# Attention scores on F32R row strips, with both first-pass chunks of a slot back to back

## The reference

```python
mod = (silu(c) @ wmod)                      # shift, scale, gate of each half
h = layernorm(x) * (1 + ca) + sa
x = x + ga * attention0(h, k0, v0, Wq, Wo)  # 16 heads of 16, 1024 queries, 4096 given keys
h = layernorm(x) * (1 + cb) + sb
x = x + gb * experts_low(h)
# second layer, modulated again
h = layernorm(x) * (1 + ca) + sa
x = x + ga * attention1(h, Wqkv, Wproj)     # 16 heads of 16, 1024 queries, 1024 keys made from h
x = x + gb * (wide attention and experts of high precision)(h)

scores = einsum('bqhd,khd->bhqk', Q, K) * SCALE
out = einsum('bhqk,khd->bqhd', softmax(scores), V)
```

## Time and profile before

| | us |
|---|---|
| runs: median, lowest, highest of 3 | 2120.23, 2119.72, 2126.68 |
| the profiled execution, by the clock of the runs | 2117.09 |
| its span in the trace | 2115.3 |
| a0's block | 69.1 to 886.4 |
| a1's block | 1035.3 to 1287 |

### The profile page before, as it was taken

One profiled execution on the slowest core, in us unless ns is written; L12 is line 12 of the kernel. 1 busy time (PEld: TensorE's weight loads), 2 busy tenths in 40 slices (PEclk: granted clock), 3 DMA queues, 4 the chain that ended last, 5 costly groups with the idle time before them and its releaser, 6 DMA issues. The chain is left out here.

```text
span 2115.3 us, 31356 instructions
## 1 busy us (share of the span) xinstructions
PE 1808.1 (85%) x9772; PEld 970.4 (46%) x9772; DVE 1399.7 (66%) x1846; ACT 1147.7 (54%) x2253; POOL 285.7 (14%) x447
## 2 busy tenths in 40 slices
PE   4499999999999999645699973499999999949997
PEld 3122222222222233133222221388888888748886
DVE  6487777877777888246467753666666666656665
ACT  3067767776777777513377762255445454424432
POOL 3210000000000000102111111211111111002223
PEclk8599999999999999856799986799999999979999
DMA  7201111111111200112312222100000000023432
GB/s 284 96 34 35 40 46 35 41 39 36 35 39 35 89 16 16 36 56 55 112 65 70 72 101 73 39 14 20 7 20 20 20 12 10 1 51 115 121 105 65
DMA packets 56274, 115.00 MB, mean 54 GB/s; under 512 B 7249, under 2 KB 21585, under 8 KB 54123
## 3 DMA queue, kind: packets, MB, share of 16 engines
q1 hardware_dynamic: 53715, 109.21, 15.9%
q10 hardware_dynamic: 2456, 4.46, 0.8%
HBM read 83.52 MB, written 30.12 MB: 54 GB/s over the span
## 5 line engine op out<-in xcount | busy, mean ns | idle before, releaser
L348 DVE TENSOR_REDUCE a_max_part<-psum 128x1 f32<-128x1024 f32 x640 | 759.6, 1220 | 253.8 <-PE psum L265 253.8
L389 ACT ACTIVATE a_probs<-psum 128x512 f32<-128x512 f32 x1280 | 675.1, 603 | 247.9 <-PE psum L309 242.7
L265 PE MATMUL psum<-a_k_rows,a_q_rows 96*128 96x512 bf16 x1280 | 399.6, 395 | 52.0 <-DMA a_q_rows<-q_parts 26.1
L309 PE MATMUL psum<-a_q_rows,a_k_rows 99*128 99x512 bf16 x1280 | 410.3, 386 | 29.6 <-ACT a_probs L389 29.3
L300 PE MATMUL psum<-a_probs,a_v_ext 128*32 128x512 f32 x2560 | 342.5, 607 | 6.1 <-ACT a_o_out L373 3.8
L265 PEld LDWEIGHTS psum<-a_k_rows,a_q_rows 96*128 96x128 bf16 x1280 | 98.8, 98 | 407.0 <-issue 193.0
L309 PEld LDWEIGHTS psum<-a_q_rows,a_k_rows 99*128 99x128 bf16 x1280 | 124.1, 98 | 268.8 <-ACT a_probs L389 155.4
L1548 PE MATMUL psum<-high_t_parts,high_gu 128*128 128x512 f32 x600 | 145.6, 393 | 6.8 <-DVE high_t_parts L1642 6.8
L1253 PE MATMUL psum<-wide_k_t,wide_q_t 128*128 128x512 f32 (+3 forms) x576 | 130.3, 353 | 1.7 <-DVE wide_id_bf L1452 1.7
L1548 PEld LDWEIGHTS psum<-high_t_parts,high_gu 128*128 128x128 f32 x600 | 113.6, 190 | 31.3 <-issue 7.3
L226 POOL TENSOR_TENSOR a_max_bf<-a_neg_max,a_zeros 128x4 bf16<-128x4 f32 x64 | 13.2, 206 | 849.0 <-DVE a_neg_max L352 849.0
(11 more groups left out here) (173 smaller groups left out, 1871.1 us busy)
## 6 DMA issues: line engine op xcount, KB each, us to landing
o<-a_o_out SPq DMA_DIRECT2D x64, 256.0 KB, 2.1
gu_in<-in_w_gu SPq DMA_DIRECT2D x25, 256.0 KB, 3.0
k_parts<-keys_parts SPq DMA_DIRECT2D x12, 512.0 KB, 6.5
a_k_rows<-k_parts SPq DMA_DIRECT2D x16, 384.0 KB
high_cw<-cw SPq DMA_DIRECT2D x24, 256.0 KB, 3.9
setup_k_in<-in_k SPq DMA_DIRECT2D x4, 1024.0 KB, 15.2
a_k_rows<-k_parts SPq DMA_DIRECT2D x16, 256.0 KB
a_v_in<-in_v SPq DMA_DIRECT2D x16, 256.0 KB, 14.8
```

The costliest lines, as they stand in the source:

```text
L265: mm = pe.matmul(psum[:, 2 * (n % 2) + j, :], q_rows[0:KROWS, b, q0:q0 + P], k_rows[0:KROWS, b, k0:k0 + 512], start=True, stop=True)
L309: pe.matmul(psum[:, bank_of(filling(j)), :], k_rows[0:SROWS, b, j * P:(j + 1) * P], q_rows[0:SROWS, b, half * QH:(half + 1) * QH], start=T ...
L348: dve.tensor_reduce(max_part[:, u % 2, c // nch, c % nch:c % nch + 1], psum[:, 2 * (n % 2):2 * (n % 2) + 2, :], AX.XY, ALU.max).then_inc(s ...
L389: act.activation(probs[:, j % pring, :], psum[:, bank_of(filling(j)), :], ACT.Exp).then_inc(exp_done, 1)
```

## The change

q and k are now held in the type F32R, in words of four bytes: each number is a high part and the rest, and three products are kept, 3 x 16 = 48 rows, with 3 rows of maxima 51. That fits twice into the array's 128 rows: strip 0 is rows 0 to 50, strip 1 rows 64 to 114, and q stands in both. Strip 0 holds the first half of the keys, strip 1 the other. A first-pass chunk is two matmuls, one on each strip (`first_half(n, 0)`, `first_half(n, 1)`); second scores take the strips in turn, j even on strip 0 and j odd on strip 1.

The order of a slot becomes S S F F S S PV. `shift` is 6 and `turn_at` 6 before the last, and the loops are unrolled. The sums are taken by VectorE instead of ScalarE, before the third reduction of the next unit. The row of maxima is written by ScalarE to a buffer of its own, and SP sends it to both strips with two DMAs. The keys come as fp32 (four DMAs a head, one for each strip's two high copies and one for its low rows) into a single buffer `k_in` and are split on GpSimd by three operations; setup does this for head 0 beside the modulation, and the split into bf16 with its stores is gone. `project` makes two parts; q stays in SBUF for a0 (`load_q` is six DMAs of 16 rows out of it), for a1 q goes through DRAM in 48 fp32 rows a head (`load_q` two DMAs) and k as it is. `nb` is 3 in a0 and 6 in a1. At unit 29 SP loads back 15 heads' sums, and `merge_heads` loads one.

```diff
+STRIP = 64
+MROWS = 3
+LOW_K, MROW = 32, 48
+SROWS = MROW + MROWS
...
-    shift = 3
-    turn_at = nkt - 2
...
+        self.shift = 6
+        self.turn_at = nkt - 6
...
+    def strip_of(self, j, rows):
+        return slice(STRIP * (j % 2), STRIP * (j % 2) + rows)
...
+    def load_k(self, sp, h):
+        keys = self.k_dram[HD * h:HD * h + HD, :]
+        for n in range(2):
+            part = keys[:, n * self.per_strip:(n + 1) * self.per_strip]
+            at = STRIP * n
+            sp.dma_start(self.k_in[at:at + 2 * HD, :],
+                         part.unsqueeze(0).broadcast_to([2, HD, self.per_strip])).then_inc(self.k_loaded, 16)
+            sp.dma_start(self.k_in[at + LOW_K:at + MROW, :], part).then_inc(self.k_loaded, 16)
...
+    def split_keys(self, pool, h):
...
+        b = h % self.nb
+        pool.wait_ge(self.k_loaded, 64 * (h + 1))
+        pool.tensor_tensor(self.k_rows[:, b, :], self.k_in[:, :], self.zeros[:, 0:1].broadcast_to([P, self.per_strip]),
+                           ALU.add).then_inc(self.k_high, 1)
+        pool.wait_ge(self.k_high, h + 1)
+        for s in range(2):
+            low = slice(STRIP * s + LOW_K, STRIP * s + MROW)
+            pool.tensor_tensor(self.k_rows[low, b, :], self.k_in[low, :], self.k_rows[low, b, :],
+                               ALU.subtract).then_inc(self.k_split, 1)
+        pool.wait_ge(self.k_split, 2 * h + 2)
...
+            def send_maxima(u):
+                b, half = (u // 2) % nb, u % 2
+                sp.wait_ge(self.row_ready, u + 1)
+                for s in range(2):
+                    sp.dma_start(q_rows[STRIP * s + MROW:STRIP * s + SROWS, b, half * QH:(half + 1) * QH].bitcast(F32),
+                                 self.max_row[0:MROWS, u % 2, :]).then_inc(self.rows_loaded[u % 2], 16)
+
+            load_q(sp, q_rows[:, 0, :], 0, self.q_loaded[0])
+            for h in range(1, nb):
+                load_q(sp, q_rows[:, h, :], h, self.q_loaded[h])
+            for h in range(1, self.early + 1):
+                sp.wait_ge(self.k_split, 2 * h)
+                self.load_k(sp, h)
+                sp.wait_ge(self.v_ready, h)
+                self.load_v(sp, h)
+            sent = self.early + 1
+            send_maxima(0)
+            for u in range(us):
+                h, half = u // 2, u % 2
+                if u + 1 < us:
+                    send_maxima(u + 1)
+                sp.wait_ge(self.o_full, u + 1)
+                sp.dma_start(self.o_dram[h, :, half * QH:(half + 1) * QH], self.o_out[:, half, :]).then_inc(self.o_stored[half], 16)
+                if half == 1 and h + nb < H:
+                    load_q(sp, q_rows[:, h % nb, :], h + nb, self.q_loaded[h % nb])
+                while sent < min(H, heads_split(u) + 1):
+                    sp.wait_ge(self.k_split, 2 * sent)
+                    self.load_k(sp, sent)
+                    sp.wait_ge(self.v_ready, sent)
+                    self.load_v(sp, sent)
+                    sent += 1
+                if u == us - 3:
+                    for n in range(2):
+                        sp.wait_ge(self.o_stored[n], 16 * (H - 1))
+                    load_sums(sp, o4, self.o_dram, 0, H - 1, self.o4_loaded)
...
+            for u in range(us):
+                if u + 1 < us:
+                    split_max(u + 1)
+                for h in range(done, heads_split(u)):
+                    self.copy_v(pool, h)
+                    self.split_keys(pool, h)
+                done = heads_split(u)
...
-                for j in range(2):
-                    k0 = ch * 1024 + j * 512
-                    mm = pe.matmul(psum[:, 2 * (n % 2) + j, :], q_rows[0:KROWS, b, q0:q0 + P],
-                                   k_rows[0:KROWS, b, k0:k0 + 512], start=True, stop=True)
-                mm.then_inc(s1_full, 1)
...
+            def first_half(n, s):
...
+                u, c = n // steps, n % steps
+                b, half, qt, ch = (u // 2) % nb, u % 2, c // self.nch, c % self.nch
+                q0, k0 = half * QH + qt * P, ch * 512
+                rows = self.strip_of(s, MROW)
+                return pe.matmul(psum[:, 2 * (n % 2) + s, :], q_rows[rows, b, q0:q0 + P], k_rows[rows, b, k0:k0 + 512],
+                                 start=True, stop=True)
...
+            def second_wait(u, j):
+                bank_free(u, self.filling(j))
+                if j == 0:
+                    pe.wait_ge(self.rows_loaded[u % 2], 32 * (u // 2 + 1))
...
+                k0, rows = (j // 2) * P, self.strip_of(j, SROWS)
+                pe.matmul(psum[:, self.bank_of(self.filling(j)), :], k_rows[rows, b, k0:k0 + P],
+                          q_rows[rows, b, half * QH:(half + 1) * QH], start=True, stop=True).then_inc(self.s2_full, 1)
...
+            def slot(u, g):
...
+                j = group * g
+                one = u * steps + 2 * g + ahead
+                for n in (j, j + 1):
+                    second_wait(u, n)
+                    second_chunk(u, n)
+                for n in (one, one + 1):
+                    if n < self.chunks:
+                        first_wait(n)
+                        first_half(n, 0)
+                        first_half(n, 1).then_inc(self.s1_full, 1)
+                if j + 2 == self.turn_at and u + 1 < us:
+                    turn_maxima(u + 1)
+                for n in (j + 2, j + 3):
+                    second_wait(u, n)
+                    second_chunk(u, n)
+                if g > 0:
+                    pv_group(u, g - 1)
+                elif u > 0:
+                    pv_group(u - 1, groups - 1)
...
+            def take_sums(u):
...
+                half = u % 2
+                dve.wait_ge(self.pv_done, (u + 1) * groups)
+                if u >= 2:
+                    dve.wait_ge(self.o_stored[half], 16 * (u // 2))
+                dve.tensor_copy(self.o_out[:, half, :], psum[:, 7, :]).then_inc(self.o_full, 1)
...
+                for s in range(steps):
+                    if s == 2 and u > 0:
+                        take_sums(u - 1)
+                    n = u * steps + s + ahead
+                    if n < self.chunks:
+                        first_pass_chunk(n)
...
-            def take_sums(it, u):
...
-                half = u % 2
-                act.wait_ge(pv_done, it * (bu * groups) + (u + 1) * groups)
-                act.wait_ge(o_stored[half], it * (16 * nb) + 16 * (u // 2 + 1))
-                act.activation(o_out[:, half, :], psum[:, 7, :], ACT.Copy).then_inc(o_full, 1)
...
+            def put_row(u):
...
+                act.wait_ge(self.turned, u + 1)
+                if u >= 2:
+                    act.wait_ge(self.rows_loaded[u % 2], 32 * (u // 2))
+                act.activation(self.max_row[0:MROWS, u % 2, :], psum[0:MROWS, self.bank_of(self.turn_at), :],
+                               ACT.Copy).then_inc(self.row_ready, 1)
...
+                def load_q(sp, rows, h, loaded):
+                    at = HD * (h % 8)
+                    for n in range(2):
+                        for m, src in enumerate((q_high, q_low, q_high)):
+                            row = STRIP * n + HD * m
+                            sp.dma_start(rows[row:row + HD, :].bitcast(F32), src[at:at + HD, h // 8, :].bitcast(F32)).then_inc(loaded, 16)
...
+                def load_q(sp, rows, h, loaded):
+                    for n in range(2):
+                        sp.dma_start(rows[STRIP * n:STRIP * n + MROW, :].bitcast(F32), q1[h, :, :]).then_inc(loaded, 16)
```

More of the change, by code:

```diff
@@ new lines, in _ @@
+            put_row(0)
+            for u in range(us):
+                for j in range(nkt):
+                    p = u * nkt + j
+                    if j == self.turn_at and u + 1 < us:
+                        put_row(u + 1)
+                    act.wait_ge(self.s2_full, p + 1)
+                    if p >= self.pring and p % group == 0:
+                        act.wait_ge(self.pv_done, (p - self.pring) // group + 1)
+                    act.activation(self.probs[:, p % self.pring, :], psum[:, self.bank_of(self.filling(j)), :],
+                                   ACT.Exp).then_inc(self.exp_done, 1)
@@ new lines, in project, with _ @@
+        if q_out is not None:
+            @block.sync
+            def _(sp):
+                heads = P // HD
+                for c in range(DC):
+                    sp.wait_ge(high_done, 2 * c + 2)
+                    sp.wait_ge(low_done, 2 * c + 2)
+                    for at, src in ((0, q_high), (HD, q_low), (2 * HD, q_high)):
+                        sp.dma_start(q_out[heads * c:heads * (c + 1), at:at + HD, :], src[:, c, :].bitcast(F32)).then_inc(stored, 16)
+                for c in range(DC):
+                    sp.wait_ge(k_taken, 2 * c + 2)
+                    sp.dma_start(k_out[c * P:(c + 1) * P, :], k_sb[:, c, :]).then_inc(stored, 16)
```

565 lines of the change are left out of this document (212 added, 353 removed).

## The result

The changed kernel takes 2273.0 us (median of 4 runs), the kernel before 2120.3: ratio 1.070, 95% interval 1.066 to 1.074. It is slower by 153, where 28 faster were forecast. One of the four runs was disturbed (3000.75) and is left out of the ratio. The two profiled spans, 2268.5 and 2115.3, differ by the same 153.2.

What follows compares the result with a forecast made beforehand. The prediction took PE (TensorE) to bound a0's slot. Its terms, a0 -97, m0 and m1 -8, p1 +2, a1 +75, sum to -28 on the profiled 2117.1: 2092 on the median's scale, range 1998 to 2157.

Steps and rivals of the forecast that it cites:

- a0's start: Front of a0: first chunk near 62.5 instead of 88.6, second scores at 97 instead of 112.2: -15 (-8 to -21).
- The strips overlap: a0's slot on PE: an F32R pair on two strips takes one matmul's time, 0.23, for a unit of 20.9.
- the lower bound by PV's column tiles: a0's slot on PE: 2.4 with pairs side by side, not 2.85, taken since PV's column tiles overlap.
- Rival A: a0's slot on PE: strips run one after another, a unit 23.9 instead of 20.9, +93, 2185; chance 0.12.
- TensorE bounds the slot before: a0's slot in the kernel before: PE is never idle in 2.83 us and sets its length.
- Just in time: a0's rows of maxima through SP: 3 us on the way, about 3.5 between the turn and the unit's end.
- hidden by 20.9: a0's queues: key and q loads stand behind the o store and are covered by a unit's 20.9 us.
- rival B: a1's queue eats a0's gain: starts wait over 10 us, clock falls to 1.2 GHz, a1 +130, 2147; chance 0.15.
- The stall before unit 31: a0's end: 15 heads' sums load at unit 29 ahead of unit 31's maxima, a stall of 18 (4 to 26).
- SP's serial queue: a1's units: maxima wait behind sums, store and loads; with start and sums load a1 loses +75 (+25 to +100).
- m0 gained, p1 lost: Outside the attentions: m0 and m1 together -8 (-10 to -4), p1's q stores +2 (0 to 3).
- The range: Whole kernel: 1998 to 2157, from the ends of the terms for a0, m0 and m1, p1 and a1.

Runs made afterwards that it cites:

- the run with rows first: Changed kernel, but SP sends unit u+2's row of maxima before it waits for unit u's sums: 2130.2 us, 1.004 of the kernel before.
- pacing: GpSimd fetches and splits one head in two units from the start, against the kernel with rows sent first: 2083.2 us, 0.982 of the kernel before.
- GpSimd's order alone: In a1 GpSimd splits a head one unit later, against the 2066.0 us kernel (rows first, paced splits, reordered start): 2010.1 us, 0.949 of the kernel before.

## Why the prediction was wrong

The forecast was 2092, the measured time 181 more. Of these, some 21 lie in a0's start, 14 in its unit (31 times 21.35 instead of 20.9), 49 in late rows and the clock behind them, 9 in a0's last unit, 8 between the attentions, 76 in a1 and 5 behind it.

- **The strips overlap: right.** The slot and the unit came nearly as worked out, 2.61 and 21.35 against 2.53 and 20.9 (20.3 to 21.5). The choice of the lower bound by PV's column tiles held. Rival A is out.
- **TensorE bounds the slot before: half right.** The slot quoted stood in the unrolled last round. In the loop most take 2.91, and 0.08 of each was order, not TensorE. It didn't change the forecast's sum, which went by the period of a unit.
- **a0's start: wrong by 20.** First chunk 69.2 instead of 62.5, second scores 117.6 instead of 97. Head 1's keys, reckoned to land 8 us after their issue, were split from 89.6 to 102.3, behind 18 q loads of 0.6 each, not 0.4. The first maxima stood behind them until 103.6 (PE waited 10.9), and the first row, which I did have queueing behind head 2's keys, was issued at 106.0 and PE waited 12.3 for it.
- **"Just in time" in a0: the step that failed first.** I put the row's way at 3 us within 3.5 of slack, and let the loads be "hidden by 20.9". At 448.2 the way was 6.3 (ScalarE's row at 441.96, two issues of 0.72 instead of 0.4, 4.2 of landing instead of 2.1), and PE left it 4.3. The loads were hidden from the engines and not from the row: it came some 2 late in 13 of 30 units, nearly every second one. The stall's second part, the granted clock at 0.50 for over eight us behind it, was in no term at all; I had it only in rival B, for a1. Together the 30 periods from the second to the last negated maximum cost 689.5, and 30 x 21.35 are 640.5: 49 us. The waits are some 27 of them (changed kernel, 150 to 820: us in total, times, longest), the rest is the clock, 2.8 in each of the eight places that had it:

```profile
PE psum L343 <- DMA a_q_rows<-a_max_row: 26.6, 13, 2.9
```

  The stall before unit 31 was 12.2, within the 4 to 26 that I gave; but here too the low clock behind it had no term, and that unit lost 24 in all beside the run with rows first.
- **a1: right mechanism, half the size.** SP's serial queue was read correctly: the row behind store and loads. It is worth 81 of a1's 151. The start was right too (second scores 30.3 behind the block's start at 1034.3, 28 to 42 reckoned). The periods were not. From unit 0's first second score (1064.6) to unit 29's (1385.5) pass 321 us, where 213 to 251 were reckoned for these 29 units: 15 to 17 where keys are loaded in each unit (8 to 11.5), 9.7 to 12.5 where keys and q take turns (7.5 to 9.5), 7.0 with the store alone (5.8 to 6.5). The sum had no term for GpSimd, though I had written down its program (maxima behind keys, keys behind a load): with rows first, pacing gave another 54, in part through SP's queue, and GpSimd's order alone 45. And I took the engines' part of a unit at the full clock, where 0.67 was granted:

```profile
1064.00:1400.00 336.00, 231.04 (x1096) 89.32 (x1096) 163.22 (x178) 148.54 (x279) 80.02 (x176) 0.67 0.16 47
```

  Rival B named this (PE's gaps bring the granted clock to 1.2 GHz, a1 +130), with a chance of 0.15, and gave 2147 because it kept a0's gain; both attentions failed by the same mechanism and I had let them fail apart.
- **m0 gained, p1 lost.** Merge and experts are 5.1 shorter, n2's first product to a1's block is 8.9 longer, where +2 was reckoned, and a1's first chunk comes 2.3 later in its block.
- **The range** was built from independent terms. A late row is one cause that acts in a0, in a1, and on the clock in both; its cases belonged in the range together.

The Trainium skill, "TensorEngine Tiling (Array Packing)", section Key Properties, says that different tiles load weights and multiply in parallel; the changed kernel's trace agrees, with four first-pass matmuls in 0.63 where four at full height take 1.03.

## What to carry to other kernels

When a value that an engine needs soon is moved into a DMA queue, list everything before it in that queue, waits and data both, and send it as soon as it exists. Where an in-order engine does background work (here the split of the keys), ask what it stands at and what urgent work is behind it; starting the background work later made this kernel faster. And count a short stall of TensorE with the clock behind it, not by its own length. Changing the order in a slot and the size of its matmuls can be worth little each and much together, when each has another resource last behind it.

## What the runs showed of the hardware that I had not expected

- A wait of 2.0 us by TensorE in a stretch at full clock was followed by the 1.2 GHz level for over eight us in which it was busy 7.78 of 8.00. Not every such wait did it: of 13 waits of 1.6 to 2.9, eight were followed by 0.50 and five, up to 2.27 long, were not. The eight cost 2.8 each on top of the wait.
- TensorE using one 64-row strip alone, 51 rows, busy without a gap, was granted 0.50 for the whole of a0; with both strips and the same numbers 1.00.
- Two 128x1024 operations of VectorE beside GpSimd's split in setup took 4.81 and 5.52 us in the changed kernel (rows below); the next one, behind GpSimd's end, took 0.69, which is also what the first form takes in the kernel before.

```profile
30.18 9.39 POOL L164 TENSOR_TENSOR a_k_rows<-a_k_in,a_k_rows 16x2048 fp32r<-16x2048 f32 x2
30.40 4.81 DVE L531 TENSOR_SCALAR setup_sign<-mod_row 128x1024 f32<-128x1024 f32 x1
...
35.14 5.52 DVE L532 SCALAR_TENSOR_TENSOR setup_size<-mod_row 128x1024 f32<-128x1024 f32 x1
...
40.69 0.69 DVE L534 TENSOR_SCALAR setup_sign<-setup_sign 128x1024 f32<-128x1024 f32 x1
```
